# The scale of the exponential in a register of ScalarE instead of a column in memory

## What is computed

```python
x = x + 0.5 * _L0_ffn_ref(_layernorm(x), ln1_w, ln1_b, w_qkv, w_proj, ln2_w, ln2_b, gate_w, gate_b, w1, w2)
x = x + _L0_attn_ref(_layernorm(x), w_qkv, w_proj, b_proj, rel_bias_table)
x = x + 0.5 * _L0_ffn_ref(_layernorm(x), ln1_w, ln1_b, w_qkv, w_proj, ln2_w, ln2_b, gate_w, gate_b, w1, w2)
```

```python
# _L0_ffn_ref(x, ...)
x = x + _msa(_layernorm(x, ln1_w, ln1_b), w_qkv, w_proj)
x = x + _moe_mlp(_layernorm(x, ln2_w, ln2_b), gate_w, gate_b, w1, w2)
# _L0_attn_ref(x, ...)
scores = jnp.einsum('bhqd,bhkd->bhqk', q, k) * scale
scores = scores + compute_bias(N, N, rel_bias_table)
attn = jax.nn.softmax(scores, axis=-1)
```

## Time and profile before

| | us |
|---|---|
| median of 3 runs | 2567.69 |
| lowest, highest | 2559.81, 2568.32 |
| the profiled execution's own time | 2557.73 |
| span of its instructions | 2555.9 |
| busy PE / ACT / DVE / POOL in that span | 2320.7 / 2139.6 / 1941.3 / 786.5 |

### The profile page before, as it was taken

One profiled execution on the slowest core, in us unless ns is written; L12 is line 12 of the kernel. 1 busy time (PEld: TensorE's weight loads), 2 busy tenths in 40 slices (PEclk: granted clock), 3 DMA queues, 4 the chain that ended last, 5 costly groups with the idle time before them and its releaser, 6 DMA issues. The chain is left out here.

```text
span 2555.9 us, 62350 instructions
## 1 busy us (share of the span) xinstructions
PE 2320.7 (91%) x24162; PEld 823.2 (32%) x24162; DVE 1941.3 (76%) x3222; ACT 2139.6 (84%) x3561; POOL 786.5 (31%) x1167
## 2 busy tenths in 40 slices
PE   5899999899998999999999999999989989989945
PEld 1222222235422324533232233222222223532434
DVE  7988898985688896577787887888988998568210
ACT  1799998999898888888888888899989999988832
POOL 1343634320633521133242022022061232062143
PEclk7899998999999999999999899999989999998967
DMA  4334423135214345642432333111101103622525
GB/s 118 95 95 143 128 76 101 42 99 174 49 35 116 110 119 167 181 108 77 114 110 84 108 97 86 46 31 40 26 22 40 31 19 99 175 56 54 134 73 150
DMA packets 269674, 231.91 MB, mean 91 GB/s; under 512 B 64241, under 2 KB 223857, under 8 KB 269346
## 3 DMA queue, kind: packets, MB, share of 16 engines
q1 hardware_dynamic: 258114, 219.54, 30.4%
q0 software_dynamic: 11264, 8.40, 1.9%
HBM read 175.35 MB, written 65.04 MB: 94 GB/s over the span
## 5 line engine op out<-in xcount | busy, mean ns | idle before, releaser
L1299 ACT ACTIVATE probs<-psum,scales 128x512 f32<-128x512 f32 x3072 | 1865.4, 723 | 215.0 <-PE psum L1066 116.2
L1410 DVE TENSOR_REDUCE maxes<-psum 128x2 f32<-128x1024 f32 x1216 | 1426.2, 1218 | 319.9 <-PE psum L1034 315.8
L1066 PE MATMUL psum<-q_staged,k_staged 27*128 27x512 f16 x3072 | 970.4, 402 | 67.2 <-ACT probs L1299 49.1
L1103 PE MATMUL psum<-probs,v_ones 128*9 128x256 f32 (+1 forms) x11520 | 993.7, 419 | 0.0
L1034 PE MATMUL psum<-k_staged,q_staged 24*128 24x512 f16 x3072 | 625.8, 405 | 69.7 <-DVE maxes L1410 51.4
L1415 DVE CUSTOM_DVE_ANT_0 biased<-psum,strips 128x512 bf16<-128x512 f32 x640 | 409.9, 686 | 117.0 <-PE psum L1034 104.1
L1034 PEld LDWEIGHTS psum<-k_staged,q_staged 24*128 24x128 f16 x3072 | 145.6, 92 | 789.0 <-issue 362.7
L1066 PEld LDWEIGHTS psum<-q_staged,k_staged 27*128 27x128 f16 x3072 | 247.7, 91 | 337.3 <-ACT probs L1299 297.2
L1103 PEld LDWEIGHTS psum<-probs,v_ones 128*9 128x9 f32 x11520 | 172.3, 89 | 327.4 <-issue 261.3
L815 POOL TENSOR_SCALAR max_rest<-max_turned 128x32 f32<-128x32 f32 x96 | 28.3, 294 | 686.7 <-DVE max_turned L1453 684.4
L1086 PE MATMUL psum<-near,ident_b 64*64 64x256 bf16 (+4 forms) x3840 | 149.7, 252 | 0.0
(11 more groups left out here) (166 smaller groups left out, 1291.3 us busy)
## 6 DMA issues: line engine op xcount, KB each, us to landing
m_w<-in_w SPq DMA_DIRECT2D x204, 256.0 KB, 3.3
near<-bias_near SPq DMA_DIRECT2D x128, 240.0 KB, 3.4
strips<-bias_strips SPq DMA_DIRECT2D x64, 288.0 KB, 3.2
k_staged<-k_parts SPq DMA_DIRECT2D x192, 48.0 KB
bias_cuts<-bias_window SPq DMA_DIRECT2D x32, 240.0 KB, 3.2
near<-bias_cuts SPq DMA_DIRECT2D x32, 240.0 KB, 3.6
bias_near<-near SPq DMA_DIRECT2D x32, 240.0 KB, 3.6
heads<-heads_t SPq DMA_DIRECT2D x384, 18.0 KB
```

Source lines behind the costliest of these rows:

```text
L1066: mm_ = pe.matmul(bank[:, :], k.kst[p][rows_, kt * P:(kt + 1) * P], queries, start=True, stop=not biased_)
L1103: last = pe.matmul(heads_bank[32 * j:32 * j + VC, columns], k.v[:, batch_of(u) * KT + kt, u % QUADS * 4 + j, :], probs[:, step % 3 * 4 + j ...
L1299: act.activation(probs[:, step % 3 * 4 + e % 4, :], bank[:, :], ACT.Exp, scale=scales[is_mid(u)][:, 3:4]).then_inc(taken, 1)
L1410: dve.reduce_max(maxes[u % 2][:, half, 2 * i:2 * i + 2, t, chunk], slot, AX.X).then_inc(drained, 1)
```

## The change

The scale of the exponential is no more an operand in memory but a register of ACT. Two registers, `unscale0` and `unscale1`, are loaded once each by `act_scales` from the fourth value of the row of scales on partition 0, behind the copy that was there; each load has a wait for `scale_row[mid]`, the semaphore that DVE's last write to that row raises. L1299 takes the register as its scale. The row has two tiles now, one for each kind of stage, where one tile was written twice. The other three scales are still spread and copied, and the copies of queries and keys (L1322) still use their columns.

```diff
-    powers, scale_of = k.sb("powers", [1, 8], I32), k.sb("scale_row", [1, 4])
+    powers, scale_of = k.sb("powers", [1, 8], I32), [k.sb(f"scale_row{mid}", [1, 4]) for mid in range(2)]
...
-        pe.matmul(scale_bank, one_row[:, :], scale_of[:, 0:4], start=True, stop=True).then_inc(scales_mm[mid], 1)
+        pe.matmul(scale_bank, one_row[:, :], scale_of[mid][:, 0:4], start=True, stop=True).then_inc(scales_mm[mid], 1)
...
-        act.activation(probs[:, step % 3 * 4 + e % 4, :], bank[:, :], ACT.Exp, scale=scales[is_mid(u)][:, 3:4]).then_inc(taken, 1)
+        act.activation(probs[:, step % 3 * 4 + e % 4, :], bank[:, :], ACT.Exp, scale=unscale[is_mid(u)]).then_inc(taken, 1)
...
         act.activation(scales[mid][:, :], scale_bank, ACT.Copy).then_inc(scales_ready[mid], 1)
+        act.wait_ge(scale_row[mid], 1)
+        act.reg_load(unscale[mid], scale_of[mid][0:1, 3:4].bitcast(I32))
...
-        dve_link(dve, dve.tensor_tensor(scale_of[:, 3:4], sized[:, 2:3], sized[:, 3:4], op=ALU.mult))
-        dve.tensor_tensor(scale_of[:, 2:3], sized[:, 0:1], sized[:, 1:2], op=ALU.mult).then_inc(scale_row[mid], 1)
+        dve_link(dve, dve.tensor_tensor(scale_of[mid][:, 3:4], sized[:, 2:3], sized[:, 3:4], op=ALU.mult))
+        dve.tensor_tensor(scale_of[mid][:, 2:3], sized[:, 0:1], sized[:, 1:2], op=ALU.mult).then_inc(scale_row[mid], 1)
...
+    unscale = [nc.scalar.alloc_register(f"unscale{mid}") for mid in range(2)]
```

More of the change, by code:

```diff
@@ L1580, in dve_powers @@
         sized = powers[:, 2:6].bitcast(F32)
-        dve_link(dve, dve.tensor_scalar(scale_of[:, 0:1], sized[:, 0:1], SCALE, None, op0=ALU.mult))
-        dve_link(dve, dve.tensor_copy(scale_of[:, 1:2], sized[:, 1:2]))
-        dve_link(dve, dve.tensor_tensor(scale_of[:, 3:4], sized[:, 2:3], sized[:, 3:4], op=ALU.mult))
-        dve.tensor_tensor(scale_of[:, 2:3], sized[:, 0:1], sized[:, 1:2], op=ALU.mult).then_inc(scale_row[mid], 1)
+        dve_link(dve, dve.tensor_scalar(scale_of[mid][:, 0:1], sized[:, 0:1], SCALE, None, op0=ALU.mult))
+        dve_link(dve, dve.tensor_copy(scale_of[mid][:, 1:2], sized[:, 1:2]))
+        dve_link(dve, dve.tensor_tensor(scale_of[mid][:, 3:4], sized[:, 2:3], sized[:, 3:4], op=ALU.mult))
+        dve.tensor_tensor(scale_of[mid][:, 2:3], sized[:, 0:1], sized[:, 1:2], op=ALU.mult).then_inc(scale_row[mid], 1)
     def dve_scale_table(dve):
```

## The result

| | before | changed |
|---|---|---|
| median | 2568.01 us of 4 runs | 2484.36 us of 4 runs |
| lowest, highest | 2559.81, 2577.53 | 2475.82, 2488.31 |
| the profiled execution, and its span | 2557.73, 2555.9 | 2486.23, 2484.4 |
| granted clock in that span | 0.933 | 0.924 |

The ratio is 0.9669 [0.9626, 0.9711]: the change saves 84 us, 3.3%. The forecast was 2460 (2395 to 2535).

The account below looks back on a forecast made before the run. ACT was taken as the bound in quiet half units without bias, DVE close behind; with bias, a loop through one exponential. Terms 22 + 32 + 27 + 28 + 6 - 9 = 106 us off 2567.7 gave 2462, forecast 2460 (2395 to 2535).

Parts of the forecast that it names:

- The price of a column: Each of 3072 exponentials on ACT saves 87 ns if a register counts as a constant; 267 us of ACT's time.
- The two loads of the register: In ACT's queue before the first exponential: 0.6 us together, nothing on the path, under 1 us even unhidden.
- Light half units: 31 groups of eight steps without bias or other work: 0.7 us each until DVE binds, 22 us.
- Half units with a projection or an output: 24 without bias at 1.35 us each, 32 us; three projection steps from 3.34 to 3.0, other five 0.3. With bias: eleven.
- Near bias: 320 half steps in the stage with bias: the loop through one exponential gets 87 ns shorter, 28 us.
- The trips: 34 expert-layer trips of 13.14 us: ten of twelve exponentials at ACT's pace, 0.8 us each, 27 us.
- Given back by the row maxima: PE's waits for the maxima's DMA come due earlier in shorter steps: about 25 waits and 9 us lost.
- The granted clock: Mean 0.933 with short falls to 1.2 GHz; left unchanged in the forecast, may move the result 20 us either way.
- The register as no constant: Exponentials on ACT take as long as with a column: no saving, 2568 us; chance 0.08.
- The slower case: Register fetched on ACT's path at every exponential, 152 ns each: 2742 us, some 85% of 206 us on the path; chance 0.07.
- ACT's slack pays further: Stalls after heads copies vanish with half the low-clock stretches; projections fall to DVE's pace: gains 140 to 190 us; chance 0.15.
- the second rival: DVE, PE and maxima DMA take nearly all, ACT's floor exceeds 490 ns, or clock is low: gains 25 to 65 us; chance 0.15.

Follow-up runs that it names:

- the third batch: Runs of four kernels: register reloaded before every exponential, two experts' output tiles on the changed kernel and on the one before, changed kernel again; kernel before 2562.86 us.
- the first batch: Runs of four kernels: constant scale, register plus bias column, two columns, shorter reductions after the change; kernel before 2563.56 us.

## Why the prediction was right, and where it was not

**The price of a column: right.** It was read as 87 ns from two forms of instruction; it measures 91 in duration and 89 from end to end in a run without gaps. Register as constant, with 0 for the fetch: right, shown by the kernel with the constant. The estimate by the Trainium skill's absolute figures (same section as above), which would have left 55 ns and 67 us, does not hold here, and the choice for the trace's 490 ns was the right one. The L1299 group fell to 601 ns and not to about 635, since the forecast took the mean for the price plus something fixed; the part of it that is waiting behind the predecessor went too.

**The two loads of the register: right.** They stand in ACT's queue at 12 and 28 us, long before the first exponential at 73 us.

```profile
L1388 ACTq TENSOR_LOAD <-scale_row x2: 287/374/461, 12.4 to 28.3; - x2
```

**Light half units: right.** "ACT's 18.92 us of a window of 19.00 become about 16.1, so DVE's 18.17 is next": 0.7 forecast, 0.78 measured at full clock, and DVE gapless at 18.20. That DVE is the bound there is shown from both sides by the two kernels with shorter reductions. ACT's part of the sentence did not come: it stands at 17.27 us of 18.20, not at 16.1. Two exponentials back to back take 0.98 us of ACT, but a pair behind a gap 1.08, and now that ACT waits for scores, more of them are of that kind (734 exponentials stand behind a gap, 485 before). So ACT has less room than forecast, and its whole busy time fell by 229.5 us and not by 267.

**Half units with a projection or an output: the size right by luck, the split wrong.** 1.35 forecast, 1.30 at full clock. The forecast let three steps with a projection fall from 3.34 to 3.0 us each and the other five bring 0.3. Two such steps of the changed kernel, at full clock, to be put beside the earlier trace rows:

```profile
124.33 1.13 PE L1168 MATMUL psum<-p_yt,w_qkv_ffn 128*128 128x512 f32 x2
...
127.58 1.12 PE L1168 MATMUL psum<-p_yt,w_qkv_ffn 128*128 128x512 f32 x2
```

They are 3.25 us apart, so such a step gave 0.1 and not 0.34, and it was the other steps that gave some 1.0. All 24 brought 16.6 us and not 32; the time at 1.2 GHz in them rose from 75 to 98 us.

**Near bias: right.** "Near half steps of 1.5 us" was the sign to look for. Two of them in ACT's timeline of the changed kernel, to be put beside the earlier trace rows:

```profile
1244.29 1.08 ACT L1299 ACTIVATE probs<-psum 128x512 f32<-128x512 f32 x2 [0.40 <-PE psum L1086]
1245.77 1.08 ACT L1299 ACTIVATE probs<-psum 128x512 f32<-128x512 f32 x2 [0.40 <-PE psum L1086]
```

The pair takes 1.08 us and not 1.26, the idle time that the bias matmuls end is 0.40, and the period is 1.48 us. It is not the same pair as in the earlier trace rows; over all pairs of that kind that follow one another (239 before, 227 after) the median period fell from 1.574 to 1.485 us. The loop keeps its form and loses one exponential's column, not two. Over a half unit: forecast 0.87 for the ten half steps of a half unit, measured 0.73 in the light ones and 1.20 (forecast with the projection 1.4) in the others. The sum of the stage is 26.5 us, with the time at 1.2 GHz in its light half units up from 51 to 61 us; the register in this stage alone gives 1.14% of 2574.78, 29 us, beside the forecast 34 and some trips.

**The trips: over-priced.** "I take 0.8: 34 x 0.8 = 27" was the step that failed. The half units with trips brought 12.8 + 2.8 = 15.6 us, about 0.5 a trip. Trip by trip, where both traces have it at full clock (24 of them), the distance from one first product to the next fell by 0.62 us in the median but by 0.44 in the mean. I had ten of twelve exponentials at ACT's pace and no one behind it. Here are three first products of the changed kernel, then one row of ACT in the first of the two trips and one of DVE in the second:

```profile
2109.23 2.94 PE L1235 MATMUL psum<-m_yt,m_w 128*128 128x128 f32 x24
...
2122.52 2.72 PE L1235 MATMUL psum<-m_yt,m_w 128*128 128x128 f32 x22
...
2135.22 2.94 PE L1235 MATMUL psum<-m_yt,m_w 128*128 128x128 f32 x24
```

```profile
2116.98 0.49 ACT L1396 ACTIVATE m_out<-psum 128x384 f32<-128x384 f32 x1 [1.77 <-DMA expert_out<-m_out]
```

```profile
2129.68 6.14 DVE L1412 TENSOR_REDUCE maxes<-psum 128x2 f32<-128x1024 f32 x5 [2.63 <-PE psum L1034]
```

The end of the second trip before the change, and the reductions in it:

```profile
2198.29 1.76 PE psum L1235 x14
```

```profile
2192.34 2.36 DVE L1410 TENSOR_REDUCE maxes<-psum 128x2 f32<-128x1024 f32 x2 [2.90 <-PE psum L1034]
2194.86 3.88 DVE L1410 TENSOR_REDUCE maxes<-psum 128x2 f32<-128x1024 f32 x3 [0.16 <-PE psum L1034]
```

With the earlier trace rows the two trips took 13.14 and 13.32 us before the change; now they take 13.29 and 12.70. The first is no shorter at all, because ACT stands 1.77 us for the store of the output. In the second DVE runs through five reductions without a gap, where it did two and three with 0.16 us between them before, so it takes over as in the light half units. Two tiles take the wait away: the first trip falls to 12.38, the second stays at 12.70, and 25 trips at full clock are 0.68 us shorter than before in the mean (0.66 in the median). Of the 0.36 us a trip that the forecast had too much, the store is some 0.24; that DVE is the other 0.12 fits these rows and was not tested by itself.

**Given back by the row maxima: right, and loose.** Forecast 9 us. The wait of PE's weight loads grew by 3.9 us in the profiled execution, from 19.4 to 23.3. In two more traces it is 29.8 (the changed kernel again) and 32.0 (the constant), so 4 to 13 us more than before.

**The granted clock: "I change nothing for it" was too easy.** In the third batch seventeen runs of the kernel before have 0.931 to 0.940, median 0.934, and five of the changed kernel 0.927 to 0.932, median 0.929. In the kernel before, 2570.42 us goes with 0.931 and 2557.73 with 0.940, some 14 us for 0.01, so 0.005 is an estimated 7 us of the missing gain. Part of this is arithmetic: the 338 us at 1.2 GHz that a clock of 0.934 makes would alone give 0.932 in the shorter span; the rest is 13 us more, 351. In the first batch the kernel with the constant has no more of them than the kernel before (339 beside 343). The profiled execution at 0.924 lost more than 7 us; another trace of the changed kernel has 249 us at 1.2 GHz in the loop beside 263 and 228, and its half units sum to about 83 us less than before the change. Whether the changed kernel is at 1.2 GHz more often as a rule, and why, was not settled, and the relation is loose: the five runs in the third batch show no order in their times.

Taken together: 115 us were forecast ahead of the maxima, 98 are there by the prices at full clock, and 13 of the 17 between them are the trips (27 + 2.6 forecast, 13.3 + 2.8 measured). From 98 to the 73.0 of the profiled pair there are the waits for the maxima and 35 us more at 1.2 GHz. The trace of the constant bears this out: 216 us at 1.2 GHz in the loop, no more than before, 12.6 us more of waits for the maxima, and half units that sum to 86.0 us less, 98 less the 12.6. By the medians of the runs the gain is 84.

**The rivals.** The register as no constant is out (0.9648 beside 0.9669). The slower case is out: the distance of two exponentials is the same even where the load itself is repeated 3072 times. Its 85% on the path was also wrong; two columns show 59%. That ACT's slack pays further is out: the gain is not 140 us, and the time at 1.2 GHz in the loop did not halve (263, 249 and 216 us in three traces with the register or a constant, 228 before). Of the second rival one part is true, DVE as next in line, and perhaps a clock that is low more often, but not so far that the gain fell to its 65 us.

## What to carry to other kernels

Count the column operands of the instruction that sets the pace: each is about 91 ns of every ACT instruction over 128x512 (the second 89 to 93), and a value that is the same for all partitions can stand in a register or in the instruction instead. Price such a saving stage by stage and only down to the next engine (here 31% of 267 us was left), and look in the trips with other work for a buffer that a faster engine will wait for. Take the price of an instruction from its shortest durations or from two forms that differ in one operand, not from the mean of a saturated group.

## What the runs showed of the hardware

- A register as the scale of an ACT instruction costs nothing over a constant: 585 ns shortest beside 586, 601 mean beside 600.
- A load of a register from memory in ACT's queue takes 270 ns at its shortest and 275 in the median; 3072 of them, one before each exponential, lengthen the kernel by 14 us of the 845 that they take; each is done at least 0.05 us ahead of its exponential, mostly beneath the one before.
- Columns add up: 476 to 494, 570 and 663 ns from start to start back to back with none, one and two; 489, 578 and 670 from end to end.
- The mean duration on a saturated engine falls by more than the price of what is taken out: 122 ns for a column of 91. In a run of 27 without a gap the recorded durations climb from 678 to 897 ns.
- With the cheaper exponential the mean granted clock is a little lower in one batch, median 0.934 to 0.929 over 17 and 5 runs; 0.002 of it is the same time at 1.2 GHz in a shorter span. Whether the rest is a rule is open.
